# A decoder block, software-pipelined by hand: one transposition by DMA instead of TensorE, one copy from VectorE to ScalarE, new orders and PSUM banks

## What is computed

```python
# 1: linear attention with random features, 16 heads of 16, 64 features
q, k, v = split(x @ Wq.T + bq), split(x @ Wk.T + bk), split(x @ Wv.T + bv)
phi = lambda z: (exp(z @ orf.T / dk**0.25 - sum(z*z) / (2*sqrt(dk))) + 1e-6) / sqrt(64)
out = (phi(q) @ (phi(k).T @ v)) / (phi(q) @ phi(k).sum(0))
x1 = layernorm(x + out @ Wo.T + bo)
# 2: softmax cross-attention with a context, 16 heads
x2 = layernorm(x1 + softmax((x1 Wk)(ctx Wq).T / 4) @ (ctx Wv))   # as the reference names its operands
# 3: feed-forward layer with ternary weights and rows rounded to 8 bits
xq = round(x2 * 127 / max|x2|);  h = silu(xq @ gate.T) * (xq @ up.T)
y  = layernorm(x2 + round(h * 127 / max|h|) @ down.T)
```

## Time and profile before

| what | value |
|---|---|
| median of three runs | 498.72 us (497.75 to 500.34) |
| the profiled execution | 497.68 us, span 496.0 us |
| busy over the span: PE, DVE, ACT, POOL | 88%, 89%, 86%, 80% |
| weight loads (PEld) | 61% |
| DMA, q1 (SP's queue) | 64.5% of 16 engines |
| mean granted TensorE clock | 0.971 |

### The profile page before, as it was taken

How to read it: one execution, slowest core, us unless ns; L and a number is a source line. 1 busy time by engine, 2 the same in 40 slices (tenths; PEclk the granted TensorE clock), 3 DMA queues, 4 the chain that set the end, 5 groups by cost and what they waited for, 6 DMA issues and landing times.

```text
span 496.0 us, 18418 instructions
## 1 busy us (share of the span) xinstructions
PE 436.3 (88%) x6535; PEld 303.5 (61%) x6566; DVE 443.3 (89%) x1291; ACT 424.1 (86%) x876; POOL 398.7 (80%) x885
## 2 busy tenths in 40 slices
PE   5577898999999999999999999999999989876641
PEld 3345565676777776777777777777776766543310
DVE  7875766999999999999999999999999989998771
ACT  3357787999999999999999999999999998977632
POOL 3499767888998998999999999999998986765423
PEclk9899999999999999999999999999999999999875
DMA  7846877777887878666666666666656868542212
GB/s 214 273 66 128 141 118 120 124 136 133 118 165 126 138 130 152 136 141 139 146 144 140 140 148 148 148 148 139 137 124 124 140 137 131 98 77 66 53 33 63
DMA packets 192659, 64.27 MB, mean 130 GB/s; under 512 B 172384, under 2 KB 192352, under 8 KB 192608
## 3 DMA queue, kind: packets, MB, share of 16 engines
q1 hardware_dynamic: 192432, 63.60, 64.5%
q10 hardware_dynamic: 176, 0.01, 0.0%
HBM read 17.31 MB, written 4.19 MB: 43 GB/s over the span
## 4 chain that ended last, share of the span: by engine, by line
DVE 36%; PE 24%; POOL 12%; DMA 10%; issue 10%; ACT 5%; SPq 2%; DVEq 0%; POOLq 0%; ACTq 0%
DVE hmax L1102 4%; DVE hh L1099 4%; PE bank L1359 4%; DVE negm L1051 4%; DVE g L1095 3%; DVE negm L1050 3%; DMA tT<-pkT 3%; POOL pkA L501 2%; PE bank L1713 2%; DMA hqT<-hq 2%; PE bank L1749 2%; DMA pkAT<-pkA 2%; PE bank L1551 2%; DMA ffn_ld<-in_L_ffn_w_down_dram 2%; PE bank L1659 2%
## 5 line engine op out<-in xcount | busy, mean ns | idle before, releaser
L1359 PE MATMUL bank<-wq_hi,xT 128*128 128x512 f16 (+1 forms) x256 | 72.0, 337 | 1.8 <-ACT xT L634 1.5
L514 POOL TENSOR_TENSOR rs<-ve,mhalf 128x1 f32<-128x1 f32 x96 | 53.0, 552 | 0.0
L1095 DVE SCALAR_TENSOR_TENSOR g<-th,bank 128x512 f32<-128x512 f32 x64 | 43.5, 679 | 5.2 <-ACT th L766 4.4
L1050 DVE TENSOR_REDUCE negm<-bank 128x4 f16<-128x512 f32 x64 | 42.8, 669 | 4.8 <-PE bank L1581 3.6
L742 ACT ACTIVATE pT<-bank 128x512 f32<-128x512 f32 x64 | 39.2, 612 | 7.0 <-PE bank L1630 4.9
L673 ACT ACTIVATE x<-y,nmr,rs 128x256 f32<-128x256 f32 x64 | 39.5, 618 | 5.8 <-DVE y L1156 3.1
L1051 DVE TENSOR_REDUCE negm<-bank 128x4 f16<-128x512 f32 x64 | 43.5, 680 | 0.0
L693 ACT ACTIVATE phq<-bank 128x512 f32<-128x512 f32 x64 | 39.0, 622 | 5.1 <-PE bank L1393 5.1
L1359 PE MATMUL bank<-wq_lo,xT 128*128 128x256 f16 (+1 forms) x128 | 42.9, 335 | 0.0
L1102 DVE TENSOR_REDUCE hmax<-hh 128x1 f32<-128x512 f32 x64 | 42.8, 680 | 0.0
L1099 DVE TENSOR_TENSOR hh<-g,bank 128x512 f32<-128x512 f32 x64 | 42.4, 674 | 0.0
(11 more groups left out here) (184 smaller groups left out, 1570.3 us busy)
## 6 DMA issues: line engine op xcount, KB each, us to landing
xs<-in_x_dram SPq DMA_DIRECT2D x32, 128.0 KB, 2.2
xr<-in_x_dram SPq DMA_DIRECT2D x32, 128.0 KB, 2.2
cs<-in_ctx_dram SPq DMA_DIRECT2D x32, 128.0 KB, 2.3
out_dram<-ot SPq DMA_DIRECT2D x32, 128.0 KB, 2.0
ffn_ld<-in_L_ffn_w_gate_dram SPq DMA_DIRECT2D x1, 1024.0 KB, 8.8
ffn_ld<-in_L_ffn_w_up_dram SPq DMA_DIRECT2D x1, 1024.0 KB, 6.1
ffn_ld<-in_L_ffn_w_down_dram SPq DMA_DIRECT2D x1, 1024.0 KB, 8.2
pkAT<-pkA SPq DMA_TRANSPOSE x64, 3.1
```

Of the source, the lines that this page charges most:

```text
L514: g.tensor_tensor(rs[n - 1][:, :], ve[n - 1][:, :], mhalf[:, :], ALU.pow).then_inc(done[f"pw{n}"], 1)
L1050: v.tensor_reduce(negm[:, 0, cols], even.rearrange("p (c t) -> p c t", c=4), AX, ALU.max, negate=True)
L1095: v.scalar_tensor_tensor(g1[:, n, :], th[:, n, :], 1.0, gate, ALU.add, ALU.mult).then_inc(done[f"gl{n}"], 1)
L1359: last = T.matmul(o, xT[:, 2 * part + c, :], w[:, c, cols], start=(n == 0), stop=(n == 5))
```

## The change

Four things are changed together.

1. The rounded rows xq are transposed by a DMA on SP's queue (`xqT_` is now a step of SP, lag 8) straight into xqT, which has two buffers. `xqTp` on TensorE and the copy on ScalarE are gone; `g0` waits for the landing.
2. `aT`, the copy of the transposed attention result from PSUM to SBUF, is on ScalarE and no longer on VectorE.
3. The orders of all five engines are new, in ramp, iteration and drain. Some lags move by one with the place where an iteration is cut.
4. Nearly all PSUM banks are dealt anew, and with them the waits of a writer for the last reader of its bank.

```diff
-        xqT = sb("xqT", [P, 2, P], BF16)
+        xqT = sb("xqT", [P, 2, 2, P], BF16)
@@ banks (part)
-        at_u1 = pb[1][:, :]
+        at_u1 = pb[3][:, :]
-        at_s1b = pb[6][:, :]
+        at_s1b = pb[1][:, :]
-        at_s0b = pb[7][:, :]
+        at_s0b = pb[3][:, :]
-        at_s1a = pb[7][:, :]
+        at_s1a = pb[3][:, :]
         at_u0 = pb[3][:, :]
-        at_xq = pb[2][:, 0:128]
@@ SP
             def load_r(t, par):
+                wait(sp, "xb", t, -2)
             def load_c(t, par):
+                wait(sp, "clo", t, -2)
+            def xqT_(t, par):
+                wait_ahead(sp, t, par, ("xqf", 0))
+                transpose(xqT[:, par, :, :], xq[:, par, :], "xqT", par)
@@ SP, iteration, new order and lags
+ store 12, load_c 3, cT_ 5, xqT_ 8, load_x 0, kT 2, hqT_ 9, qT 2, row 6, load_r 2, tT_ 5
@@ GpSimd, iteration, new order
+ xqf 8, nlo 2, lo 2, rs1 5, hq1 9, hq0 9, ya2 7, xhi 0, xlo 0, phe 3, rs2 7, nf 1, rs3 10, chi 4, clo 4,
+ xb_ 3, nhi 1, qnt 7
@@ ScalarE
+            def aT(t, par):
+                wait(act, "aTp", t)
+                copy(attT[:, :, :], at_aT.rearrange("p (c t) -> p c t", c=2), "aT")
-            def xqT_(t, par):
-                wait(act, "xqTp", t)
-                copy(xqT[:, :, :], at_xq.bitcast(BF16).rearrange("p (c t) -> p c t", c=2), "xqT")
@@ VectorE
-            def aT(t, par):
-                wait(dve, "aTp", t)
-                v.tensor_copy(attT[:, :, :], at_aT.rearrange("p (c t) -> p c t", c=2)).then_inc(done["aT"], 1)
@@ VectorE, iteration, new order
+ sd 9, tlo 5, ad3 9, hu1 8, hh0 8, am 7, hh1 8, nr 1, ac 7, hx 8, ar 7, hc 8, bs3 9, ad1 4, hr 8, rd 3, hs 8,
+ bs1 4, at 3, sg 7, y1 4, m0 5, qk_ 0, rx 6, y3 9, oxn 6, m1 5, vsm 2, bs2 6, gl0 7, kve 2, hu0 7, y2 6, v_ 0, gl1 7
@@ TensorE, new waits in the loop (writer of a bank for its last reader)
+ s0: wait_looped "ad1", t+1      s1: wait_looped "ephk0", t+3 and "m0", t     u0: wait_looped "m1", t+2
+ u1: wait_looped "hu0", t        mTp: "ephq0", t+3    tm: "kve", t+2          oxp: "at", t+3
+ g0: wait_looped "qk", t+7 (was at xqTp) and wait_moved "xqT"
-            def xqTp(t, par):
-                wait(pe, "xqf", t)
-                for k in range(2):
-                    last = T.transpose(dst[:, k * P:(k + 1) * P], xq[:, par, k * P:(k + 1) * P], idb[:, :])
@@ TensorE, iteration, new order
+ kvp 3, xTp 0, dn 9, u1 8, nump 3, st1 6, st0 6, phk0 2, ntp 3, phk1 2, wo 4, pv1 6, pv0 6, s0 5, qkm 0,
+ phq0 2, phq1 2, oxp 6, s1 5, g0 7, vhp 5, kvs 2, g1_ 7, u0 7, mTp 5, x1Tp 4, vm 0, tm 4, aTp 3
```

More of the change, by code:

```diff
@@ L425, in drain @@
[L425 to L429, removed]
+                trail(hqT_, i, -208, 21)
+                trail(qT, i, -215, 28)
+                trail(row, i, -211, 24)
+                trail(load_x, i, -264, 30)
+                trail(load_r, i, -214, 28)
+                trail(load_c, i, -214, 27)
@@ L574, in ramp @@
[L574 to L580, removed]
+                lead(hq0, i, -40, 5)
+                lead(hq1, i, -40, 5)
+                once(late_constants, i, -48)
+                lead(ya2, i, -42, 7)
+                lead(xhi, i, -49, 14)
+                lead(xlo, i, -49, 14)
@@ new lines, in ramp @@
+                lead(phe, i, -46, 11)
+                lead(rs2, i, -42, 7)
+                lead(chi, i, -45, 10)
+                lead(nf, i, -48, 13)
+                lead(clo, i, -45, 10)
+                lead(xb_, i, -46, 11)
+                lead(rs3, i, -39, 4)
+                lead(nhi, i, -48, 13)
+                lead(qnt, i, -42, 7)
+                lead(xqf, i, -42, 6)
+                lead(nlo, i, -48, 12)
+                lead(lo, i, -48, 12)
+                lead(rs1, i, -45, 9)
@@ new lines, in ramp @@
+                once(ternaries[3], i, -21)
+                lead(kvs, i, -24, 10)
+                lead(g1_, i, -19, 5)
+                if i == -20:
+                    pe.wait_ge(done["qk"], 7)
+                once(ternaries[5], i, -20)
+                lead(u0, i, -19, 5)
+                lead(mTp, i, -21, 7)
+                lead(x1Tp, i, -22, 8)
+                lead(vm, i, -26, 12)
+                lead(tm, i, -22, 8)
+                lead(kvp, i, -24, 9)
+                lead(xTp, i, -27, 12)
@@ new lines, in ramp @@
+                once(ternaries[2], i, -22)
+                lead(phk1, i, -25, 10)
+                lead(ntp, i, -24, 9)
+                lead(phk0, i, -25, 10)
+                lead(pv1, i, -21, 6)
+                lead(pv0, i, -21, 6)
+                lead(s0, i, -22, 7)
+                lead(qkm, i, -27, 12)
+                lead(phq1, i, -25, 10)
+                if i == -21:
+                    pe.wait_ge(done["ephk1"], 5)
+                once(ternaries[4], i, -21)
+                lead(oxp, i, -21, 6)
@@ L1868, in _ @@
-            run(pe, ramp, iteration, drain, (-40, -9), 14, 30, (-3, 8))
+                go(tm, i, par, 4)
+                go(aTp, i, par, 3)
+            def drain(i):
+                trail(nump, i, -40, 27)
+                trail(st1, i, -37, 24)
+                trail(st0, i, -37, 24)
+                trail(phk0, i, -41, 28)
+                trail(wo, i, -39, 26)
+                trail(ntp, i, -40, 27)
+                trail(phk1, i, -41, 28)
+                trail(xTp, i, -43, 30)
+                trail(pv1, i, -37, 24)
+                trail(pv0, i, -37, 24)
+                trail(s0, i, -38, 25)
+                trail(qkm, i, -43, 30)
+                trail(phq1, i, -41, 28)
+                trail(oxp, i, -37, 24)
+                trail(phq0, i, -41, 28)
+                trail(s1, i, -38, 25)
+                trail(g0, i, -36, 23)
+                trail(g1_, i, -36, 23)
+                trail(kvs, i, -41, 28)
+                trail(u0, i, -36, 23)
+                trail(mTp, i, -38, 25)
+                trail(x1Tp, i, -39, 26)
+                trail(vhp, i, -38, 25)
+                trail(vm, i, -43, 30)
+                trail(aTp, i, -40, 27)
+                trail(tm, i, -39, 26)
+                trail(kvp, i, -41, 27)
+                trail(dn, i, -35, 21)
+                trail(u1, i, -36, 22)
```

1109 lines of the change are left out of this document (547 added, 562 removed), and 10 rows, old and new, of the table done.

## The result

The changed kernel takes 505.44 us in the median of four runs (504.80 to 508.91), the kernel before 498.27 beside it; the ratio is 1.0116 (95% interval 1.0079 to 1.0153). It is slower by 1.2%, where 493.5 and a gain were forecast, and outside the range. The profiled execution took 505.27 us for a span of 503.3, 7.3 us more than before.

| us | before | after | difference |
|---|---|---|---|
| first `qk_` | 12.6 | 18.7 | +6.1 |
| `qk_` of tile 8 | 95.5 | 95.7 | +0.2 |
| `qk_` of tile 16 | 201.9 | 205.1 | +3.2 |
| turn in the loop (tiles 16 to 29, over 13) | 12.90 | 12.98 | +0.08 |
| `qk_` of tile 29 | 369.7 | 373.8 | +4.1 |

The account below looks back on a forecast made before the run. VectorE was taken to bound the kernel at 12.9 us a turn. Loop -2.9, unrolled tiles -2.4, drain -0.6, fill -1.5 and tail +2 made -5.4 us, giving a forecast of 493.5 us, range 485.5 to 501.5.

Parts of the forecast that it names:

- VectorE thus sets the 12.9 us: In the loop before, VectorE's own work was claimed to set the 12.9 us turn, with GpSimd level to 0.2.
- The 12.45: VectorE's own sum a turn in the loop, from 12.90 to 12.57 without `aT`, and 12.45 without the `lo` wait.
- worth 0.1 either way: On TensorE, parting `phk0`, `ntp`, `phk1` and joining `st1`, `st0` was put at 0.1 us, gain or loss.
- the 12.95: Failure test for the loop: the prediction fails if the turn is over 12.95 us; 12.6 to 12.8 was expected.
- The two closed paths: Loops of bank hand-overs between TensorE and VectorE, each 12.7 us, capping the new turn at 12.72, 0.18 less than before.
- the first path: `qk_` releases `g0`, TensorE runs to `dn` (5.4 us), VectorE from `ad3` to `qk_` (7.1); with two hand-overs 12.7.
- SP's queue: A sixth transpose on SP, 1.5 us a turn, was to bring its work from 10.7 to 12.2 and cost nothing.
- The eight unrolled tiles: Tiles before the loop, claimed to gain 0.3 us each, 2.4 in all, partly from less pkA lateness.
- Fill and tail: Start and end of the kernel: fill -1.5 us (+3 to -5), tail +2 (0 to +7) for about three exposed tiles.
- A: Rival: VectorE's sum alone is the bound, loop turn 12.57 or less, span 489.5 down to 486 us; chance 0.14.
- B: Rival: exposed DMA transposition eats the gain (500.5 us), or ScalarE or TensorE holds the turn at 12.85 (497.5); chance 0.22.
- C: Rival: bank holds of TensorE at `s1`, `g0`, `u0`, `u1` cost 0.1 us more each, turn 13.1, 503.6 us; chance 0.17.

Follow-up runs that it names:

- experiment 10: Kernel before with VectorE's `tlo` replaced by a tiny memset (VectorE 0.25 us less a turn): 499.27 us (0.9995), turn 12.92.
- 2: Changed kernel with the copy `aT` back on VectorE, between `tlo` and `ad3`: 505.72 us (1.0115), turn 12.99.
- 5: Changed kernel with two of six matmuls left out of `qkm` (0.44 us of TensorE a tile): 499.37 us (1.0015), turn 12.87.
- 6: Changed kernel with `phk1` directly behind `phk0` and `ntp` behind both in the loop: 504.32 us (1.0108), turn 12.89.
- 8: Changed kernel with xq transposed by TensorE and copied by ScalarE again, in all tiles: 515.73 us (1.0336); second kernel, last nine tiles only: 525.96 us (1.0530).
- experiment 7: Changed kernel with the DMA transposition of xq in the last nine tiles left out: 501.86 us (1.0061); issued twice: 515.19 us (1.0317).

## Why the prediction failed

**The step that failed** is the first one, "VectorE thus sets the 12.9 us", with "TensorE close behind" left without a sum. VectorE had next to no idle time and the chain ran along it, but that didn't make it the bound. Taking 0.25 us from it in the kernel before left the turn at 12.92 (experiment 10), and giving the copy back after left it at 12.99 (2). What held the turn before is, by the rows, a closed path over three engines; no run has shown it. (The 12.45 for VectorE without the wait for `lo` was mis-taken as well: the wait is 0.8 us in ten turns, which gives 12.49.)

**The term that replaced the gain** is TensorE's. I took 0.12 us off it for `xqTp` and booked the new places at nothing ("worth 0.1 either way"). From 12.90 that would be 12.78 at the most; its string came out at 12.98. Here are the distances from start to start in the two timelines, means of nine turns. Dearer are `phk0`, `ntp`, `phk1` by 0.10, `oxp` by 0.09, `tm` by 0.05 and `wo` by 0.04. Cheaper are `xqTp` by its 0.12, `vhp`, `s1`, `vm` and `g0` together by 0.08 (with `tm`'s hold for x1T in them) and the two `phq` by 0.03. That is the 0.08 of the turn to within rounding. The turn was over the 12.95 at which I had said that the prediction fails; experiments 5, 6 and 8 together show TensorE as its bound.

**The two closed paths** were the right kind of thing and the wrong two. With `qkm` cut, which neither holds, the turn fell (5); with `phk1` moved and with `xqTp` back, which neither holds, it changed too (6, 8). Before the change I had put the first path "some 1 us shorter than the turn" and looked for no other; a third was tight.

**SP's queue:** right in size and in the loop (1.42 us for 1.5; waits of 6.1 us in ten turns, so 12.4 of work for 12.2), wrong outside it. The eight unrolled tiles were to gain 2.4 and lost 3.0. There `hqT` and xqT landed late, 4.5 us in four waits. I had costed `qT`'s earlier landing but not `hqT` behind the new transpose. But the loss varies: four kernels whose instructions are the same up to there (the changed one, both of experiment 7 and the second of 8) had `qk_` of tile 16 at 202.0 to 206.8 and took 106.4 to 109.4 us for the eight tiles, where the kernel before took 106.4. The 3.0 are the largest of the four. With the transposition on TensorE in all tiles the stretch took 110.7. So the late landings are an account of one execution and not a shown cause, and what sets the size of a stall was not tried.

**Fill and tail:** the late first `qk_` was made up as said, without the 1.5 of gain. The tail was +3.2 for +2: mechanism right (three tiles exposed, 2.4 to 3.2 us for 0.92), and 3.0 of it are the transposition (7); the 1.3 a tile that `ad3`'s new place was to give back did not come, for without the transposition the rest is no shorter than before.

**Of the rivals,** A (VectorE alone) is excluded. B had the exposed transposition and a turn held at 12.85 by TensorE; its mechanisms came true, both at once and at 12.98, and I had priced them only one at a time. C had the sign and nearly the size (503.6) by another cause: none of its four holds of a bank shows a pause on TensorE in the loop. A weight load of L1727 waits for `m1` (0.3 us a turn), but the matmuls of `u0` follow those of `g1_` without a gap. Only with 0.44 us less on TensorE does a hold of C's show, `s1`'s (5).

None of the kernels tried beats the kernel before.

## What to carry to other kernels

When every engine is full, relieve each in turn (leave out an instruction or two) before trusting a chain of waits: a relief that gives nothing says more than a busy share of 99%. If none gives, look for the closed path over several engines, and count a moved step by what it delays on that path, not by its engine's sum. A transposition by DMA that is free in a full loop is paid in the drain, where its landing lies on the chain (3.0 us here); weigh it there. And before a short pause of TensorE is read as one, count the matmuls of its line against their weight loads: a missing record looks like idle time.

## What the hardware showed that was not expected

A step's place among TensorE's matmuls has a price without any wait: moving `phk1` ahead of `ntp` took 0.09 off the turn, and `oxp` takes 0.44 us with `phq1` behind it and 0.53 with `s1` behind it, though the profile marks no wait of TensorE's matmuls there (what makes the difference was not tried). The queue is held almost as long by a transposition of 64 KB (1.17 us) as by one of 256 KB (1.24 in the same turn), and the landing took 2.3 against 2.8 us: in this turn the number of issues counts, hardly their bytes. In the unrolled stretch single issues of the same transpositions took far longer, in both kernels (2.53 us for pkA at 193.62 after, 2.35 for hq at 124.18 before); what stretches them was not tried.
